# Attention on one core: the logits of the pair eight steps back move behind row logits, turns and products with v

## The reference

```python
q = (x @ Wq).reshape(b, n, 32, 16)
k, v = jnp.split(ctx @ Wkv, 2, axis=-1)
q = apply_axial_rope(q, pos_map); k = apply_axial_rope(k, ctx_pos_map)
logits = jnp.einsum('bqhd,bkhd->bhqk', q, k) / 4
w = jax.nn.softmax(logits, axis=-1)
attn = jnp.einsum('bhqk,bkhd->bqhd', w, v).reshape(b, n, 512)
x = x + attn @ Wout + bout
```

## Time and profile before

| what | value |
|---|---|
| time, median of 3 runs | 1368.52 us (1367.78 to 1371.84) |
| the profiled execution | 1368.46 us, span 1366.6 us |
| mean granted clock of the tensor engine | 0.995 of full |
| PE busy | 1323.9 us, 97% |
| VectorE (DVE) busy | 824.1 us, 60% |
| ScalarE (ACT) busy | 486.6 us, 36% |
| cross-attention | about 346 to 711 us of the span |

### The profile page before, as it was taken

One profiled execution on the slowest core, in us unless ns is written; L12 is line 12 of the kernel. 1 busy time (PEld: TensorE's weight loads), 2 busy tenths in 40 slices (PEclk: granted clock), 3 DMA queues, 4 the chain that ended last, 5 costly groups with the idle time before them and its releaser, 6 DMA issues. The chain is left out here.

```text
span 1366.6 us, 24155 instructions
## 1 busy us (share of the span) xinstructions
PE 1323.9 (97%) x8490; PEld 1072.5 (78%) x8490; DVE 824.1 (60%) x1495; ACT 486.6 (36%) x766; POOL 521.4 (38%) x371
## 2 busy tenths in 40 slices
PE   8999999998699999999999999999999999999997
PEld 7777888877567777777567788888888899999986
DVE  6766667789687888888844657555531222222248
ACT  4222333334266665666665111111101232222221
POOL 1122221225453443444142008441133687565074
PEclk9999999999899999999999999999999999999999
DMA  7993000002755545555400003230010544453257
GB/s 270 317 319 119 0 0 0 0 7 92 198 155 162 175 142 152 152 161 166 133 1 23 24 24 146 85 150 24 23 39 1 193 144 148 145 174 112 78 178 246
DMA packets 84796, 159.84 MB, mean 117 GB/s; under 512 B 8208, under 2 KB 61584, under 8 KB 81424
## 3 DMA queue, kind: packets, MB, share of 16 engines
q1 hardware_dynamic: 78448, 124.19, 29.0%
q0 software_dynamic: 6272, 34.61, 7.2%
HBM read 109.22 MB, written 69.47 MB: 131 GB/s over the span
## 5 line engine op out<-in xcount | busy, mean ns | idle before, releaser
L1477 DVE TENSOR_REDUCE b_mx<-b_rt 128x4 f32<-128x1024 f32 x128 | 156.0, 1221 | 36.5 <-PE b_rt L1260 35.8
L1637 ACT ACTIVATE b_pf<-b_rt,b_zero 128x1024 f32<-128x1024 f32 x128 | 142.9, 1116 | 98.6 <-PE b_rt L1274 98.0
L2198 DVE SCALAR_TENSOR_TENSOR residual<-c_yp,c_shared,residual 128x512 f32<-128x512 f32 x128 | 92.3, 745 | 104.7 <-PE c_yp L43 100.6
L41 PE MATMUL c_fc<-c_xh,c_w 128*128 128x512 f32 x348 | 136.0, 391 | 0.0
L43 PE MATMUL c_fc<-c_xh,c_w 128*128 128x512 f32 x348 | 135.5, 389 | 0.0
L42 PE MATMUL c_fc<-c_xl,c_w 128*128 128x512 f32 x348 | 135.4, 389 | 0.0
L2362 ACT ACTIVATE c_s<-c_fc 128x512 f32<-128x512 f32 x43 | 25.7, 598 | 228.0 <-PE c_fc L43 217.0
L2212 DVE TENSOR_TENSOR c_hTl<-c_eh,c_hTh 128x384 fp32r<-128x384 f32 x39 | 21.7, 557 | 139.1 <-ACT c_hTh L2386 135.6
L41 PE MATMUL c_fc<-c_ring,c_xTl 128*128 x312 | 104.1, 334 | 0.0
L43 PE MATMUL c_fc<-c_ring,c_xTh 128*128 x312 | 100.6, 322 | 0.0
L42 PE MATMUL c_fc<-c_ring,c_xTh 128*128 x312 | 100.3, 321 | 0.0
(11 more groups left out here) (451 smaller groups left out, 3534.4 us busy)
## 6 DMA issues: line engine op xcount, KB each, us to landing
weights_b<-b_pack SPq DMA_DIRECT2D x128, 200.0 KB
c_eraw<-in_c_we POOLq DMA_DIRECT2D x8, 2176.0 KB, 9.6
b_pack<-b_hi SPq DMA_DIRECT2D x56, 256.0 KB, 2.5
c_rows_in<-in_b_ctx SPq DMA_DIRECT2D x39, 256.0 KB, 11.0
c_rows_out<-in_b_ctx SPq DMA_DIRECT2D x39, 256.0 KB, 11.0
c_xe<-c_rows_in SPq DMA_DIRECT2D x39, 256.0 KB, 2.7
c_rows_out<-c_ye SPq DMA_DIRECT2D x39, 256.0 KB
c_wraw<-in_c_ws SPq DMA_DIRECT2D x11, 768.0 KB, 4.3
```

The source lines that it names most:

```text
L41: nc.tensor.matmul(out, ll, rh, start=start, stop=False)
L1477: nc.vector.tensor_reduce(out=mx[:, :, 2 * p:2 * p + 2].rearrange("p t e -> p e t"), in_=rt[:, row_bank(g, p):row_bank(g, p) + 2, :].rearr ...
L1637: nc.scalar.activation(pf[:, s:s + 2, :], rt[:, 2:4, :], ACT.Exp, scale=XD ** -0.5, bias=zero[:, :]).then_inc(e_done, 1)
L2198: nc.vector.scalar_tensor_tensor(out=X[:, t, :], in0=yp[:, (n * 4 + k) % 3, :], scalar=shared[:, t:t + 1], in1=X[:, t, :], op0=ALU.mult, o ...
```

## The change

On the tensor engine, and there alone, the loop that issues `logits` moves within each step. Before, it stood first, ahead of `rows`. After, it stands behind `rows`, the turns and `values`, just ahead of the piece of projection. No instruction is added or removed, and the waits move with the instructions that have them.

```diff
             def body(b, live):
                 for i in range(T):
-                    for d, p in pairs(i, live, LAGS):
-                        logits(b + d, p)
                     for d, p in pairs(i, live, 0):
                         rows(b + d, p)
...
                     for d, q in quads(i, live, LAGV):
                         values(b + d, q)
+                    for d, p in pairs(i, live, LAGS):
+                        logits(b + d, p)
                     for step, what, n, parts in PLAN:
                         for d in due(i, live, step):
                             if not (fresh(b + d) and step < 0):
```

## The result

The change makes the kernel slower: 1438.49 us (median of 4 runs, 1437.06 to 1439.7) against 1368.47 us (4 runs, 1367.78 to 1371.84), a ratio of 1.0491 (95% interval 1.0472 to 1.0511), 70 us. The forecast was 1418 us, range 1398 to 1433. The direction is right, the size too small by 20 us, and the time lies above the range.

What follows compares the result with a forecast made beforehand. The prediction took PE's own list of work to bound the attention stage. Its terms, 36 + 6 + 4.6 + 3 = 50 us, on 1368.46 us gave 1418 us, with a range of 1398 to 1433 us.

Steps and rivals of the forecast that it cites:

- What bounds the kernel: Attention stage: PE's own list of work sets the pace, and every microsecond won or lost passes to the end.
- The full batch: Each of six full batches of 16 steps takes 6.0 us more, 36 us in all.
- Splits: Separating logits from row logits adds changes of shape that drain PE: 4.2 us a full batch (3.4 to 4.7).
- the waits taken away: Logits now stand between row logits and what made PE wait for DVE: 0.5 us a full batch back.
- the entry from the turns into logits: Even steps: a new change of shape from turns to logits, bounded by 0 and 0.17 us, taken as 0.10.
- Late exponential: ACT's copies and casts queue behind it, and DVE behind ACT: 1.5 + 0.15 + 0.6 us a full batch.
- The steps without projections: Longer waits cost 6 us in the last batch and 4.6 us in about eight early steps; clock stays 1.00.
- The tail: Last eight steps, no row logits: turns wait for the late copy, 0.75 us for each of four pairs, 3 us.
- A: Rival: only PE's drains count and the chain through ACT is hidden, 31 us more, 1399 us; chance 0.18.
- B: Rival: waits add up until most steps run to the ACT loop, 0.15 us more per step, 1436 us; chance 0.11.
- C: Rival: drains are hidden and row logits no longer stand behind an exponential, 7 us faster, 1361 us; chance 0.03.
- D: Rival: no difference, since PE runs the list so far ahead that order does not matter; chance 0.03.

Runs made afterwards that it cites:

- e1: The changed kernel, but in each step the scalar engine copies the maxima and the products with v before it takes the exponential; 1407.3 us.
- e4: The kernel before, with the row logits instead of the logits moved behind the turns and the products with v; 1408.9 us.
- e6: The kernel before, with logits and row logits both moved, together, behind the turns or products with v and ahead of the projection; 1439.7 us.
- e7: As e6, and the scalar engine also copies the maxima and the products with v before it takes the exponential; 1412.3 us.
- e9: The changed kernel with 5 needless turns of the identity ahead of the row logits in steps with little or no projection; 1428.8 us.
- e5: The kernel before, with the late logits only in batches 0, 1, 7 and what follows, the old order in batches 2 to 6; 1401.5 us.
- e8: The kernel before, with row logits put ahead of logits, the two still together and first in the step; 1371.2 us.
- e10: The kernel before, with late logits only in the last eight steps, behind the last row logits; 1388.9 us.

## Why the prediction was right in direction and wrong in size

*What bounds the kernel*: right. PE's list sets the pace, and what was added to it came out at the end.

*The full batch*: right in its sum, 6.0 us forecast and 6.08 measured, but with some luck, for two errors cancel. Splits: the forecast has 4.2 for the drains less 0.5 for the waits taken away, 3.7 in all, and e1, which has both, measures 4.7. From R to R an odd step costs 0.20 us more than before, as forecast (0.21), an even one 0.40 in place of 0.31: the entry from the turns into logits costs the 0.17 us of the earlier trace rows or a little more, not the 0.10 taken between the bounds, and little came back of the 0.5. Late exponential: 1.5 + 0.15 + 0.6 = 2.25 forecast against 49.63 - 48.24 = 1.4. Against e1, step 8 costs 0.72 us (forecast 0.70) and steps 2, 10 and 14 cost 0.20 each (0.19), but step 12 costs 0.27 in place of 0.4, step 5 nothing in place of 0.2, and step 4 is 0.22 quicker. A change of shape behind L or R has this price in every order: 0.44 us in after, e1 and e4, and 0.23 only inside the united pair of e6 and e7. The Trainium skill's "TensorEngine Tiling (Array Packing)", section Key Properties, says that changing the tiling mode drains TensorE, and gives no price. The trace agrees, with these 0.44 against 0.23 us.

*The steps without projections*: the step that failed. The prediction says of the clock that "the rows show 1.00 across the stretch with idle time, so I don't count on that", and so it puts the clock's part at nothing. The rows showed 1.00 for idle time of 2.7 us in many short pieces. The change makes of it waits of 0.8 to 1.2 us in most pairs of steps, and at about 398 and 709 us, in a V that had waited 1.2 us for the maxima, the clock goes to 0.50. In the last batch this is at least 9.35 us (e9 against after) of the 17.3, at the start at least 2.65 of the 3.9 above the forecast: 12 of the 19 us that the profiled execution lies above the sum. The waits themselves were sized about right. At full clock the first pair takes 4.3 us (702.86 to 707.19) where 4.2 was forecast, and the first three pairs of e5, one of them with the maxima's copy, take 13.9 us, where the forecast's prices give 4.2 + 5.6 + 4.2 = 14.0 and before has 11.5.

*The tail*: mechanism right, size wrong. I had bounded the wait for the copy at 0.6 to 1.5 us and took 0.75 for each of four; after's five waits of L1295 there are 0.58, 1.47, 1.47, 1.47 and 0.49 us, 5.5 together against 1.0 before. R127 to the next stage is 4.75 us longer, not 3; the remaining 1.65 us of the row are in the feed-forward.

*Rivals*: A (drains only, 1399) is what e1 comes near, 1407. In e1's profiled execution 33.6 of the 39.3 us above before are in attention, against A's 31, and 5.7 are in the feed-forward, which the edit does not touch. e4, 1409, has 39.5 us in attention, with its own waits in them. B's 1436 is near the time, but not for its reason: 0.15 us more in every step would make a full batch of about 52 us, and it takes 49.63; nor did R's waits for DVE grow (1.5 us in six, 1.8 in six before). That 1438 stands so near to 1436 is chance. C and D are out; e8 shows that even with the pair united, R first gains nothing.

The sum then: 30.4 (five batches, splits 23.5, late exponential 7) + 1.2 + 13.4 at the start + 17.3 in the last batch, of the last two 2.65 and 9.35 at least the clock, + 4.75 + 1.65 = 68.7 us. None of the twelve kernels beats the one before.

## What to carry to other kernels

When a change turns many short idle pieces of the tensor engine into a few waits of a microsecond, price the stretch at both clock levels: a clock of 1.00 over the idle time of before is no evidence for longer gaps, and once it has fallen it can stay there for tens of microseconds (37 here). Ask what stands behind a delayed instruction in its consumer's queue: 31 of 70 us here, those of the clock among them, came from two kinds of copies queued behind a late exponential, and putting them first removed them without touching the tensor engine. Splitting two groups of the same shape costs 0.2 to 0.4 us in every step of a full pipeline, whichever of the two moves. And when a sum comes out, check its terms one by one: here two errors of about 1 us a batch hid each other.

## What the runs showed of the hardware

- In after the clock fell to 0.50 at about 709 us and stayed there to 746.5, in spite of PE being busy for 9.62 of 9.66 us from 726.24 to 735.90. In e5, in the same steps, it came back after 4.58 us without idle time. What brings it back is open. Work without any use (e9) makes the stretch 9.35 us shorter.
- When it falls is open as well: e4 has 4.85 us of idle time in its 26.24 us from R115 to R127 and stays at 1.00, e5 is idle for 5.1 of the first 14.9 us before the clock falls, after for 2.2 of 6.1.
- The same waits (1.47 us, three times in the tail) stand before a fall of the clock in e10 and not in after. What decides between them is open.
- e6 falls below 1.00 also in full batches, with 3.7 us of idle time in 50.9.
- Open as well: the profiled executions of e9 and e10 lost some 13 us in the feed-forward (662.7 and 661.6 us from its first turn to the end, 648.3 before), which neither edit touches. In e10 part of it is at 1312 to 1342 us of the span, where PE is busy for 24.03 of 30 us at a clock of 0.83, behind an ACT cast that started late with no cause in the trace:

```profile
1317.54 0.48 ACT L2390 CAST c_hTh<-c_eh 128x384 fp32r<-128x384 f32 x1 [4.38 <-remote]
...
1318.05 0.56 DVE L2216 TENSOR_TENSOR c_hTl<-c_eh,c_hTh 128x384 fp32r<-128x384 f32 x1 [6.34 <-ACT c_hTh L2390]
```

e1, on another chip, lost 5.7 us there as well. The kernel before reached 1381 us on the chip of e9 and e10, so it may be spread from one execution to the next; no run was made to tell.
